# Two buffers per chunk, by the parity of the node pair, for the sums of convolutions that end in row statistics

## The reference, cut to what matters

```python
def _layernorm(x, axis=-1, eps=1e-05):
    m = jnp.mean(x, axis=axis, keepdims=True)
    v = jnp.var(x, axis=axis, keepdims=True)
    return (x - m) / jnp.sqrt(v + eps)
...
    x = _layernorm(x + _L1_gnn_ref(...), axis=-1)      # ends with eve convolution 2
    x = _layernorm(x + _L2_gnn_ref(...), axis=-1)      # ends with sage convolution 2
```

## Time and profile before

| what | us |
|---|---|
| median of 3 runs | 11201.85 |
| the three runs | 11162.76, 11201.85, 11206.03 |
| the profiled execution, its own time | 11186.57 |
| its span, first to last instruction | 11184.0 |
| m5 (eve 2, norm), 5664 to 6838 | 1174 |
| m7 (sage 2, norm), 7879 to 8919 | 1040 |
| m4 (eve 1, relu), 4637 to 5663 | 1026 |
| m6 (sage 1, swish), 6838 to 7878 | 1040 |

### The profile page before, as it was taken

How to read it: one execution, slowest core, us unless ns; L and a number is a source line. 1 busy time by engine, 2 the same in 40 slices (tenths; PEclk the granted TensorE clock), 3 DMA queues, 4 the chain that set the end, 5 groups by cost and what they waited for, 6 DMA issues and landing times. The chain is left out here.

```text
span 11184.0 us, 167613 instructions
## 1 busy us (share of the span) xinstructions
PE 6640.9 (59%) x37142; PEld 5031.2 (45%) x37143; DVE 6252.3 (56%) x16776; ACT 4592.8 (41%) x8654; POOL 7206.7 (64%) x7581
## 2 busy tenths in 40 slices
PE   1004776677567679877768885544577554444443
PEld 1004665566566653355545554544455432222221
DVE  3335665566566656444445554333465467777776
ACT  1111221233233335444445553333455546666665
POOL 3657776777677720377766665777677675666562
PEclk9999888888799989899989997777788776667766
DMA  5997887899799978677767776777798733333332
GB/s 138 225 200 228 282 272 240 291 340 321 239 337 331 326 256 283 208 260 264 246 223 266 266 260 200 267 253 248 246 316 301 254 94 106 110 115 102 100 107 73
DMA packets 1864868, 2570.07 MB, mean 230 GB/s; under 512 B 255773, under 2 KB 1369141, under 8 KB 1864662
## 3 DMA queue, kind: packets, MB, share of 16 engines
q1 hardware_dynamic: 1134168, 1627.27, 44.1%
q10 hardware_dynamic: 504726, 564.87, 15.4%
q0 software_dynamic: 225792, 375.94, 10.8%
HBM read 1499.62 MB, written 1129.98 MB: 235 GB/s over the span
## 5 line engine op out<-in xcount | busy, mean ns | idle before, releaser
L1027 POOL DMA_INDIRECT sums_gcn<-m_result,m_idx x1176 | 1163.5, 989 | 432.3 <-issue 350.6
L1136 PE MATMUL m_n_bank<-k_ident,m_in_y 128*128 128x128 f32 x5488 | 851.9, 313 | 914.2 <-DMA m_in_y<-node_rows_c 383.3
L1019 POOL DMA_INDIRECT m_rows<-node_rows_a,m_idx x1176 | 1130.0, 961 | 339.3 <-issue 331.5
L1721 DVE TENSOR_TENSOR m_z<-m_n_bank,m_in_sums 128x512 f32<-128x512 f32 (+1 forms) x784 | 506.1, 686 | 1320.5 <-ACT m_o L1757 372.7
L1169 ACT ACTIVATE m_nodeT<-m_n_bank 128x512 f32<-128x512 f32 x980 | 534.3, 597 | 1724.5 <-PE m_n_bank L1136 1720.4
L1136 PEld LDWEIGHTS m_n_bank<-k_ident,m_in_y 128*128 128x128 f32 x5488 | 721.7, 162 | 1006.2 <-issue 816.9
L1027 POOL DMA_INDIRECT sums_eve<-m_result,m_idx x784 | 762.6, 973 | 415.5 <-issue 230.0
L1027 POOL DMA_INDIRECT sums_sage<-m_result,m_idx x784 | 762.7, 973 | 266.3 <-issue 230.2
L1632 DVE SCALAR_TENSOR_TENSOR m_acc<-m_n_bank,m_scales,m_res_b 128x128 f32<-128x128 f32 (+1 forms) x2352 | 634.3, 343 | 496.4 <-PE m_n_bank L1154 430.2
L1019 POOL DMA_INDIRECT m_rows<-node_rows_b,m_idx x784 | 755.5, 964 | 226.1 <-issue 223.4
L1575 PE MATMUL m_gram<-m_y 128*128 128x129 f32 (+1 forms) x4800 | 681.9, 306 | 315.9 <-ACT m_y L1601 314.3
(11 more groups left out here) (296 smaller groups left out, 17441.6 us busy)
## 6 DMA issues: line engine op xcount, KB each, us to landing
m_in_sums<-sums_gcn SPq DMA_DIRECT2D x291, 512.0 KB
m_in_y<-node_rows_a SPq DMA_DIRECT2D x291, 512.0 KB
sums_gcn<-k_gcn_b SPq DMA_DIRECT2D x194, 512.0 KB
node_rows_a<-m_y ACTq DMA_DIRECT2D x194, 512.0 KB
m_in_x<-in_x_dram SPq DMA_DIRECT2D x194, 512.0 KB
m_in_y<-node_rows_b SPq DMA_DIRECT2D x194, 512.0 KB
sums_eve<-k_eve_b SPq DMA_DIRECT2D x194, 512.0 KB
m_in_sums<-sums_eve SPq DMA_DIRECT2D x194, 512.0 KB
```

The source lines that it names most:

```text
L1019: pool.indirect_dma_start(self.rows[b][:, t, :], None, self.table[:, :], bass.IndirectOffsetOnAxis(self.idx[s][:, t:t + 1], 0)).then_inc(s ...
L1027: pool.indirect_dma_start(self.node_sums[:, :], bass.IndirectOffsetOnAxis(self.idx[s][:, T + t:T + t + 1], 0), self.result[b][:, t, :], No ...
L1136: mm = pe.transpose(self.n_bank[i][:, t * P:t * P + n], self.buf["y"][i // 2][0:n, H * (i % 2) + t, :], self.k["ident"][0:n, 0:n])
L1721: dve.tensor_tensor(self.z[b][0:n, half, :], ph.node_out(i, n), ph.buf["sums"][b][0:n, half, :], ALU.add).then_inc(ph.n_out_read, 1)
```

## The change

In the norm phases z[b] becomes two buffers, chosen by the parity of the pair: DVE writes pair m into the one of m, while ACT still applies pair m-1 from the other (`last_z`). DVE's wait on `finished` ahead of each chunk is dropped there. Since scale and shift are still single, a new semaphore `applied`, raised by ACT after a pair's stores have been started, is waited for by DVE ahead of `solve_scale`. Relu and swish phases keep one buffer and the wait, and get ACT's raise of `applied`. Inside the loop the parity is known only at run time, so the address of z is computed in a register (`bass.ds(m & 1, 1)`). The memset of z at the start of a norm phase covers both buffers.

```diff
-        self.z, self.o = ([ph.sb(f"{n}{b}", [P, T, D]) for b in range(2)] for n in ("z", "o"))
+        self.turns = 2 if finish == "norm" else 1
+        self.z = [ph.sb(f"z{b}", [P, self.turns, T, D]) for b in range(2)]
+        self.o = [ph.sb(f"o{b}", [P, T, D]) for b in range(2)]
...
+        self.applied = ph.sem("applied")
+        self.grants = [(ph.nodes_turned, 2), (self.applied, 1)] + [(ph.used[n], 2) for n in ph.used] + [(s, 16) for s in ph.stored]
+
+    def z_of(self, m, b):
+        if self.turns == 1:
+            return self.z[b][:, 0, :, :]
+        if isinstance(m, int):
+            return self.z[b][:, m % 2, :, :]
+        return self.z[b][:, bass.ds(m & 1, 1), :, :].rearrange("p o t f -> p (o t) f")
...
             if i % 2 == 0:
                 ph.have(dve, "sums", m, b)
-                dve.wait_ge(ph.finished, 2 * m + b + 1)
-            dve.tensor_tensor(self.z[b][0:n, half, :], ph.node_out(i, n), ph.buf["sums"][b][0:n, half, :], ALU.add).then_inc(ph.n_out_read, 1)
+                if not norm:
+                    dve.wait_ge(ph.finished, 2 * m + b + 1)
+            dve.tensor_tensor(self.z_of(m, b)[0:n, half, :], ph.node_out(i, n), ph.buf["sums"][b][0:n, half, :], ALU.add).then_inc(ph.n_out_read, 1)
...
-                    ins = self.ln.take(dve, self.z[b], n, b * T)
+                    ins = self.ln.take(dve, self.z_of(m, b), n, b * T)
...
     def finish_vector(self, dve, m):
         if self.finish == "norm":
+            dve.wait_ge(self.applied, m + 1)
             self.ln.solve_scale(dve, m)
...
+    def last_z(self, m, b):
+        return self.z_of(m - 1 if isinstance(m, int) else m + 1, b)
...
-                self.ln.apply(act, self.o[b], self.z[b], n, b * T).then_inc(ph.finished, 1)
+                self.ln.apply(act, self.o[b], self.last_z(m, b), n, b * T).then_inc(ph.finished, 1)
...
         ph.store_before(act, m, self.o)
+        act.sem_inc(self.applied, 1)
```

More of the change, by code:

```diff
@@ L1688, in __init__ @@
             self.ln = Norm(ph, "ln", 2 * T)
-        self.grants = [(ph.nodes_turned, 2)] + [(ph.used[n], 2) for n in ph.used] + [(s, 16) for s in ph.stored]
+        self.applied = ph.sem("applied")
[6 more added lines that the diff above has]
+        return self.z[b][:, bass.ds(m & 1, 1), :, :].rearrange("p o t f -> p (o t) f")
     def tensor_start(self, pe):
@@ L1702, in vector_start @@
         for b in range(2):
-            dve.memset(self.z[b][:, :, :], 0.0).then_inc(self.z_done, 1)
+            dve.memset(self.z[b][:, :, :, :], 0.0).then_inc(self.z_done, 1)
         if self.finish == "norm":
@@ L1753, in finish_scalar @@
             if self.finish == "norm":
-                self.ln.apply(act, self.o[b], self.z[b], n, b * T).then_inc(ph.finished, 1)
+                self.ln.apply(act, self.o[b], self.last_z(m, b), n, b * T).then_inc(ph.finished, 1)
             else:
                 act.wait_ge(self.z_done, 2 * m + b + 1)
-                act.activation(self.o[b][0:n, :, :], self.z[b][0:n, :, :], ACT.Relu if self.finish == "relu" else ACT.Silu).then_inc(ph.finished, 1)
+                act.activation(self.o[b][0:n, :, :], self.last_z(m, b)[0:n, :, :], ACT.Relu if self.finish == "relu" else ACT.Silu).then_inc(ph.finished, 1)
         ph.store_before(act, m, self.o)
+        act.sem_inc(self.applied, 1)
 def run_conv(nc, ph, edges, nodes):
```

## The result

| | us |
|---|---|
| kernel before, median of 11 runs | 11183.34 (11162.76 to 11206.03) |
| changed kernel, median of 11 runs | 11234.50 (11217.77 to 11242.23) |
| ratio | 1.0043, interval 1.0036 to 1.0051 |
| predicted | 11198, range 11135 to 11250 |
| changed kernel, profiled execution and its span | 11242.23, 11240.2 |

The kernel became slower by some 48 us by the ratio, 51 us between the medians. That is inside the band of 0.5% to which the prediction gave most of its chance, but some nine times the +5.3 us of its sum.

A forecast was written before the change was run, and what follows sets the result against it. The prediction took m7 as bound by POOL and m5 by ScalarE's chain with its stores' landing. Terms -1 - 1.5 + 7.8 = +5.3 us gave 11191.9 on the profiled time, 11207 on the median; it said 11198, range 11135 to 11250.

The forecast's parts named there:

- the largest wait of the profile: VectorE's wait for z in m5: removing it gains -1 us there, as the landing covers it, and -1.5 us in m7.
- register instructions between them: Fifteen a pair between ScalarE's applications: taken as 0, since the sequencer works ahead; upper bound 116 us in m5.
- The wait for `applied`: VectorE's new wait ahead of the reciprocal: costs nothing, because ScalarE's root of the same pair ends last.
- three signs: Sixteen applications at 6.8 us or more, the landing holding the second pair less than before, or POOL's m5 waits shrinking.
- Transfers that move: SP's second load and fill start some 1.5 us earlier, at ScalarE's stores in m5: taken as 0, bounds -19 to +12.
- The registers ahead of the first application: Two more register instructions on ScalarE's chain in every pair of m5: +7.8 us; in m7 beside POOL.
- The root of the second pair: On ScalarE in m5: comes up to 0.8 us earlier, but the landing still holds the applications, so gain 0.
- Registers in the row: Rival: the sequencer can't keep ahead, so ScalarE's applications in m5 stretch; full bound +116 us, to 11303; chance 0.07.
- The wait was the bound: Rival: z's release sets the second pair, so m5 shortens until POOL binds, 134 us less, to 11053; chance 0.09.
- The transfers decide within the band: Rival: the stores' landing in m5 moves by -19 or +12 us, giving 11173 to 11204; counted within "same", chance 0.84.

The follow-up runs named there:

- e8: Changed kernel with both loads of sums held until ScalarE has issued its stores; ratio 0.9978 to the kernel before, m5 1168.4 us.
- e9: Changed kernel with both loads of sums held behind ScalarE's stores and VectorE's wait on the applications put back; ratio 0.9996, m5 1171.6 us.
- e3b: Changed kernel with each chunk's fill issued only when its store has landed; ratio 1.0050 to the kernel before, m5 1256.2 us.
- e6: Changed kernel with only the second load of sums, and the fill behind it, held until ScalarE has issued its stores; ratio 1.0002, m5 1199.8 us.
- e10: Kernel before plus an unread 512 KB load per pair of m5, issued behind the first load of sums, ahead of the stores; ratio 1.0053, m5 1259.4 us.
- e7: Kernel before, without the change, with both loads of sums held until ScalarE has issued its stores; ratio 0.9960, m5 1150.9 us.
- e5b: Kernel before with three small unread activations on ScalarE ahead of the first mix of each group of edges in m5; ratio 1.0032, m5 1226.5 us.
- e1b: Changed kernel with VectorE's wait for the application of the chunk before put back; ratio 1.0024 to the kernel before, m5 1193.1 us.
- e11: Kernel before plus an unread 512 KB load per pair of m5, issued behind the second load of sums; ratio 1.0004, m5 1201.1 us.
- e4: Kernel before with each chunk's fill issued only when its store has landed, on the chip where the kernel before took 15827.24 us; ratio 1.0013.

## Why the prediction was wrong

**Right.** m7 is bound by POOL and didn't move (1042.4 to 1040.5). m5 took 148 us more than m7 from memset to memset, where the prediction has 134; that changes nothing in it. In m5 the chain runs through ScalarE and the landing of its stores, and the largest wait of the profile, VectorE's 179.4 us for z, was worth next to nothing: with the landing out of the way m5 takes 1168.4 us without it (e8) and 1171.6 with it (e9). The sixteen applications stayed at 6.26 to 6.27 us, so register instructions between them cost nothing. The wait for `applied` doesn't show in any row of waits. None of the three signs came by which the prediction said that it would know itself wrong: they watched the rivals that it had named, and none watched a later landing.

**The step that failed: "Transfers that move".** It named the right mechanism, saw that SP's transfers would start 1.5 us earlier, "right at ScalarE's stores", and took 0 with -19 to +12 us. Measured are 92.3 - 47.6 = +44.7 us of wait, of which some 4 us (0.17 in each of 24 pairs) are the register instructions behind the landing. Three things were wrong with it.
- It took its bounds from the spread of the held pairs in the kernel before, 1.22 to 2.50 us. In 20 of 20 steady units of that trace the second load starts behind the stores. The spread of one order says nothing of the other.
- It named the load and the fill, but took 0 because of the fill alone, which overlaps the stores before and after. The load of sums just ahead of it is what crosses the stores: the two lines of SP's single issues put it 1.19 us behind them before and 0.45 ahead after, so it moved by 1.64 us, which is the 1.5 of the prediction; its start was hidden in the merged row. e3b shows that the fill isn't the cause, and e6 and e10 that a load is.
- It priced the Trainium skill's rule ("Trainium Kernel Development and Optimization", section Key Constraints) from the same spread, at +12. The rule had the right sign. An estimate by bytes would have been nearer: 512 KB at the 0.42 MB/us that the DMA engines move when full (in the changed kernel 422 GB/s from 6329.52 to 6330.52) are 1.25 us, over 24 units 30 us.

**Terms that were missing or mis-sized.**
- The edges. The prediction had nothing for what a later start of the edges does to them. Between the last store and the next root the mean of the steady units grew from 25.13 to 25.93 us, 0.80 x 20 = 16 us. TensorE waits longer for its first mix, and its granted clock in the 9 us around is lower, so that eight matmuls take 2.07 us and not 1.27. Windows and rows of PE, before and after:

```profile
6311.00:6320.00 9.00, 4.93 (x16) 2.60 (x16) 5.36 (x18) 3.48 (x7) 4.27 (x5) 0.81 0.99 359
...
6314.38 1.27 PE L1078 MATMUL m_e_out<-k_eve,m_mix 128*128 128x128 f32 x8 [3.85 <-ACT m_mix L1426]
```

```profile
6349.00:6358.00 9.00, 5.17 (x15) 3.59 (x16) 1.16 (x1) 3.47 (x7) 1.91 (x2) 0.59 1.03 412
...
6352.14 2.07 PE L1078 MATMUL m_e_out<-k_eve,m_mix 128*128 128x128 f32 x8 [5.01 <-ACT m_mix L1426]
```

  A share of 0.59 means that the lower of the two levels, 1.2 GHz, was granted for most of these 9 us, after a wait of 5.01 us. Over 20 units the mean share from 3 us ahead of the last store to 6 us behind it is 0.81 before, 0.70 after, 0.97 in e7 and 0.76 in e5b. The edges take 25.13, 25.93, 24.24 and, with the inserted 1.17 us off, 26.57 - 1.17 = 25.40 us. The order is the same. In the other nine traces it holds roughly: the share goes down to 0.64 (e10, edges 25.67 us), and the longest edges are those of the changed kernel. That the clock alone makes the difference is argued, not shown.
- The registers ahead of the first application: 0.24 us instead of 0.16 in the first pair of each unit. In the second pair the landing doesn't cover them, as they stand behind the wait for it (L1202): from the landing to the first application the median is 0.02 us before and 0.19 in the changed kernel, e1b and e6, so 0.17 us. That is 0.41 us a unit, some +10 us over 24 units against the predicted +7.8.
- The root of the second pair was to come up to 0.8 us earlier. It came later, 11.58 us behind the first root instead of 11.20 (means). ScalarE's four copies stand ahead of it and behind the stores, and start at +9.65, where before they start at +9.27; VectorE's early statistics don't bring them forward.

The parts, as means of the steady units: +0.38 us up to the second root, +1.76 from there to the last store (the landing, and 0.17 of register instructions), +0.80 in the edges, 2.94 us in all. Over the 20 units that is 59 of the 65.4 us of m5; the rest lies in the units at its ends. POOL's wait for results grew from 171.5 to 237.1 us, as much as m5.

**The rivals.** "Registers in the row" was the wrong mechanism on the right side. "The wait was the bound" is refuted by the result, where the wait is gone and m5 is longer, and by e8 and e9. "The transfers decide within the band" was the right one, with a little over a quarter of the size on the slow side (12 of 44.7 us).

**Open.** Untouched phases moved too: the attention phase took 2252 to 2258 us in the five traces with registers and free additions, 2259 to 2264 in the six without registers, 2271 and 2278 in the two with registers and the wait back. The difference is spread over the whole phase. I didn't trace it further; it is a part of why m5 lost 65 us and the kernel 48 (another is that the traced execution of the changed kernel is the slowest of its eleven), and it goes with e1b and e9 standing above what their m5 says. For e1b 27 us of the kernel's time so stay without a cause.

## What to carry to other kernels

When a change frees an engine earlier, list every transfer that the freed buffer releases, with its time against the transfers on the chain. Here a load that crossed over a store on which the chain waits cost more than its own bytes take (69 us of m5 in e10, against 30 us estimated above for 24 loads), while one that stayed behind cost little (10 us in e11); and the spread of the old order gives no bound for the new one. If loads with slack stand ahead of such a store, hold them with one semaphore until it is issued: here that was worth some 40 us. Of a long wait ask what ends last beside it, and behind a longer pause look at TensorE's granted clock as well.

## What the runs showed of the hardware

- In m5 ScalarE's stores didn't share the engines with SP's loads from their issue on: the more loads SP had issued shortly ahead, the later they began to move. With one load of 512 KB issued by SP in the 1.5 us ahead of them, the stores' first packet came 2.1 to 2.5 us after their issue, with two 3.9 to 4.2, with none 0.9 to 1.0. The Trainium skill ("DMA: Bandwidth & Descriptors", section Queues, rings and completion order) has each DMA engine alternate between the queues that have work, packet by packet. These traces show that only once the stores' packets move: in the 3 us above q10 has 2 packets against q1's 171. The Trainium skill ("Perfetto Trace Analysis", section DMA Instruction — HWDGE (DVE, Sync)) also says that the block which makes descriptors is locked for one issuer at a time; by that section a wait for the lock stands inside the issue's own row. The stores' two issues take 0.99 us before and 1.07 in the changed kernel (medians), so at most 0.08 us of the 1.5 can be that, and the cause of the order stays open.
- So each load ahead put the stores' start off by 1.2 to 1.8 us, against 1.25 us for its 512 KB at the full rate; the applications behind were delayed by more (e10: 2.8 us). Why isn't shown; SP's packets still move beside the stores' then.
- On one chip the kernel before took 15827 us instead of 11183. A trace of e4 there has VectorE standing still for up to 36 us at a time.
